# Attention of a transformer block on one core: maxima by query, probabilities by key, sums in column strips, norms once per sequence

## The reference

```python
q, k, v = heads(ln(x) @ Wq), heads(ln(x) @ Wk), heads(ln(x) @ Wv)   # 16 heads of 8 columns
scores = einsum('bhld,bhlwd->bhlw', q, k_win) * 8 ** -0.5            # keys l-63 .. l of each query l
attn = softmax(where(invalid, -inf, scores))
x = x + (einsum('bhlw,bhlwd->bhld', attn, v_win)) @ Wo
xf = ln(x)                                                           # 8192 rows
weights, experts = top_k(softmax(xf @ w_router), 2)                  # 8 experts, capacity 2048, in order of rows
y = gelu(rows_of_expert @ w1[e]) @ w2[e]                             # 128 -> 512 -> 128
out = x + bias + sum_k weights_k * y_k                               # rows over the capacity drop out
```

## Time and profile before

| | us |
|---|---|
| runs | 1155.83, 1158.16, 1158.24 (median 1158.16) |
| profiled execution, its span | 1155.7 |
| TensorE matmul busy in it | 990.6 (86%) |
| VectorE, ScalarE, POOL busy | 644.9, 609.6, 488.5 |
| mean granted TensorE clock | 0.912 |

### The profile page before, as it was taken

One profiled execution on the slowest core, in us unless ns is written; L12 is line 12 of the kernel. 1 busy time (PEld: TensorE's weight loads), 2 busy tenths in 40 slices (PEclk: granted clock), 3 DMA queues, 4 the chain that ended last, 5 costly groups with the idle time before them and its releaser, 6 DMA issues.

```text
span 1155.7 us, 24887 instructions
## 1 busy us (share of the span) xinstructions
PE 990.6 (86%) x7670; PEld 942.3 (82%) x7670; DVE 644.9 (56%) x1980; ACT 609.6 (53%) x1898; POOL 488.5 (42%) x445
## 2 busy tenths in 40 slices
PE   2999998899899889989997998999605998889791
PEld 1899998799799889988997997999604997878691
DVE  5777787488468747856774786578521121212110
ACT  2777676466467647655673765567202442434330
POOL 4122124421712352162135225212531877777777
PEclk9999999799799979988997998899656999889896
DMA  8900001100100110010011001000122455455533
GB/s 186 390 17 18 11 10 47 32 18 18 56 12 9 41 37 9 18 60 17 9 36 42 9 18 56 22 9 31 50 65 87 54 90 90 76 84 89 89 33 34
DMA packets 61821, 60.14 MB, mean 52 GB/s; under 512 B 6721, under 2 KB 50648, under 8 KB 60736
## 3 DMA queue, kind: packets, MB, share of 16 engines
q1 hardware_dynamic: 34944, 40.18, 10.6%
q0 software_dynamic: 22528, 17.22, 10.3%
q10 hardware_dynamic: 4288, 2.10, 1.2%
HBM read 17.70 MB, written 31.59 MB: 43 GB/s over the span
## 4 chain that ended last, share of the span: by engine, by line
PE 44%; issue 18%; POOL 11%; DVE 11%; another core or an unknown queue 6%; ACT 4%; DMA 3%; ACTq 1%; DVEq 1%; POOLq 0%; SPq 0%
PE bank L993 15%; PE bank L1015 11%; POOL out L429 11%; PE bank L1002 8%; PE bank L1029 2%; DMA out<-y_sb,xg 2%; ACT probs L509 2%; ACT kT L479 2%; DVE negmax L661 2%; DVE probsT L666 1%; PE bank L979 1%; PE bank L1021 1%; DVE xn L652 1%; PE bank L973 1%
## 5 line engine op out<-in xcount | busy, mean ns | idle before, releaser
L509 ACT ACTIVATE probs<-bank,negmax 128x128 f32<-128x128 f32 x1036 | 295.2, 368 | 285.2 <-DVE negmax L661 278.4
L360 POOL TENSOR_TENSOR qbd<-qT,quadmask 128x512 f32<-128x512 f32 x132 | 134.5, 1040 | 522.8 <-ACT qT L467 400.3
L993 PE MATMUL bank<-kT,qbd 128*128 (+1 forms) x2072 | 295.1, 289 | 0.0
L993 PEld LDWEIGHTS bank<-kT,qbd 128*128 128x128 f32 x2072 | 273.2, 206 | 0.0
L1015 PEld LDWEIGHTS bank<-v_sb,probsT 128*128 128x128 f32 x2048 | 263.1, 200 | 3.7 <-issue 3.4
L1015 PE MATMUL bank<-v_sb,probsT 128*128 (+1 forms) x2048 | 258.9, 259 | 3.7 <-issue 3.5
L429 POOL DMA_INDIRECT out<-y_sb,xg x128 | 198.2, 1548 | 81.0 <-DVE y_sb L934 42.0
L661 DVE TENSOR_REDUCE negmax<-bank 128x4 f32<-128x512 f32 x259 | 177.9, 687 | 75.5 <-PE bank L993 42.4
L1002 PE MATMUL bank<-ident,probs 128*128 128x128 f32 x1024 | 170.1, 291 | 39.2 <-ACT probsT L515 26.6
L666 DVE COPY probsT<-bank 128x512 f32<-128x512 f32 x192 | 132.5, 690 | 122.7 <-PE bank L1002 76.0
L1002 PEld LDWEIGHTS bank<-ident,probs 128*128 128x128 f32 x1024 | 125.0, 152 | 56.5 <-ACT probsT L515 30.6
(11 more groups left out here) (114 smaller groups left out, 930.6 us busy)
## 6 DMA issues: line engine op xcount, KB each, us to landing
slots_dram<-empty_rows SPq DMA_DIRECT2D x8, 1096.0 KB, 15.4
xg<-slots_dram SPq DMA_DIRECT2D x32, 274.0 KB, 4.3
rows_sb<-xn SPq DMA_DIRECT2D x33, 128.0 KB
out<-xbias SPq DMA_DIRECT2D x32, 128.0 KB
w_sb<-in_L_ffn_w SPq DMA_DIRECT2D x16, 256.0 KB
send_rows<-rows_sb SPq DMA_DIRECT2D x7, 548.0 KB, 3.0
out<-y_sb,xg POOLq DMA_INDIRECT x128
slots_dram<-send_rows,slot_id POOLq DMA_INDIRECT x112
```

The costliest lines, as they stand in the source:

```text
L360: last = pool.tensor_tensor(out=qbd[s][half][:, :, :, :], in0=q.unsqueeze(2).to_broadcast([P, 2, HQ, BLK]), in1=heads.to_broadcast([P, 2, ...
L509: last = nc.scalar.activation(probs[:, k % 4, c, :], scores[k % 4][:, c * P:(c + 1) * P], ACT.Exp, bias=negmax[:, k % 4, c:c + 1])
L993: last = mm(scores[k % 4][:, c * P:(c + 1) * P], qbd[s][half][:, blk, h:h + 2, :].rearrange("p h q -> p (h q)"), keys.rearrange("p o j -> ...
```

## The change

Attention now goes tile by tile (64 slots of 128 rows), and 8 tiles, a whole sequence, form a loop's body.

- Scores are computed twice. `scores` (by query) serves the maxima only: per half of the heads, two bf16 matmuls write the mask (64 rows of contraction, 512 columns), and 8 f32 matmuls with only 32 rows of contraction add the scores; neighbours in the list stand in different strips of 32 rows and write different banks. VectorE takes the maxima of 128 x 1024 in one instruction, negated, and splits them in a bf16 part and a rest (`low_part`); `maxima_T` transposes them, and `maxima_out` copies them to 32 rows of `moving`.
- `scores_T` (by key) makes the scores with keys on the partitions: 8 bf16 matmuls of 96 rows put mask and negated maxima into PSUM, and 4 f32 matmuls of 32 rows and 256 columns add the scores. ScalarE then needs one `Exp` of 128 x 1024 without a bias, and its result needs no transpose: L1002, L666 and L515 are gone.
- `weighted` has the values as stationary operand, 32 columns wide, and 128 moving columns of probabilities; four groups of heads write four strips of 32 partitions. The result is copied by ScalarE (128 x 512) and transposed back by 4 transposes (`weighted_T`).
- The norms are done once per sequence with 16 columns at a time (8 tiles of each norm); POOL does the subtraction and the product (`normed`, `normed_again`). The second norm, the router and the routing of a sequence run within the next one; `rows_sb` holds one sequence, and `keep_rows` is gone.
- `sends`: 4 indirect DMAs in each of the slots 0 to 3, two sequences later. The last two sequences' are sent after the loop.
- VectorE waits for the load of all of x (`ld_x[1]`) ahead of its first maxima.
- The experts' stage keeps its work; its tensors in PSUM have other names.

The diff, cut to its core:

```diff
-            def keep_rows(n):
-                sp.wait_ge(s_xn2, n + 1)
-                sp.dma_start(rows_sb[:, bass.ds(2 * n, 2), 0:D], xn2[:, :, :]).then_inc(s_rows, 16)
...
+            def normed_again(b):
+                pool.wait_ge(s_ln, b + 2)
+                pool.wait_ge(s_send, START + 16 * (b - 1))
+                tiles = x_sb[:, bass.ds((b - 1) * TILES, TILES), :]
+                pool.tensor_tensor(out=rows_sb[:, :, 0:D], in0=tiles,
+                                   in1=mean[:, 0:TILES].unsqueeze(2).to_broadcast([P, TILES, D]),
+                                   op=ALU.subtract).then_inc(s_xd2, 1)
+                pool.wait_ge(s_xd2, b)
+                for h in range(2):
+                    half = slice(4 * h, 4 * h + 4)
+                    pool.tensor_tensor(out=rows_sb[:, half, 0:D], in0=rows_sb[:, half, 0:D],
+                                       in1=rs_y[:, half].unsqueeze(2).to_broadcast([P, 4, D]),
+                                       op=ALU.mult).then_inc(s_xn2, 1)
+            def sends(b, t):
+                if t == 0:
+                    pool.wait_ge(s_send, START + 16 * (b - 1))
+                    pool.sem_inc(s_turn_pool, 1)
+                if t < 4:
+                    send(send_rows, range(2 * t, 2 * t + 2))
+                if t == 5:
+                    pool.wait_ge(s_scat, 16 * TOPK * TILES * (b - 1))
+                    pool.sem_inc(s_sent, 1)
...
-            def exps(n, k):
-                act.wait_ge(s_max, UNITS * n + k + 1)
-                for c in range(4):
-                    last = nc.scalar.activation(probs[:, k % 4, c, :], scores[k % 4][:, c * P:(c + 1) * P], ACT.Exp,
-                                                bias=negmax[:, k % 4, c:c + 1])
-                last.then_inc(s_exp, 1)
...
+            def exps(g, gp):
+                act.wait_ge(s_scoresT, 2 * g + gp + 1)
+                nc.scalar.activation(probsT[:, gp].rearrange("p b k h q -> p (b k h q)"),
+                                     sT_ps[:, :, :].rearrange("p b c -> p (b c)"), ACT.Exp).then_inc(s_exp, 1)
+            def weighted_out(g):
+                act.wait_ge(s_pv, 2 * g + 2)
+                nc.scalar.copy(u_sb[:, :, :].rearrange("p i q -> p (i q)"), u_ps[:, :]).then_inc(s_u, 1)
...
+            def score_max(g, gp):
+                dve.wait_ge(s_scores, 2 * g + gp + 1)
+                nc.vector.tensor_reduce(negmax[:, 0, gp * 8:gp * 8 + 8],
+                                        s_ps[:, :, :].rearrange("p b (c j) -> p (b c) j", c=4),
                                         AX.X, ALU.max, negate=True).then_inc(s_max, 1)
...
+            def low_part(g):
+                dve.wait_ge(s_max, 2 * g + 2)
+                nc.vector.tensor_copy(negmax_hi[:, :], negmax[:, 0, :]).then_inc(d_hi, 1)
+                dve.wait_ge(d_hi, g + 1)
+                nc.vector.tensor_tensor(out=negmax[:, 1, :], in0=negmax[:, 0, :], in1=negmax_hi[:, :],
+                                        op=ALU.subtract).then_inc(s_low, 1)
+            def maxima_out(g):
+                dve.wait_ge(s_maxT, g + 1)
+                nc.vector.tensor_copy(moving[0:STRIP, :, :].rearrange("p h q -> p (h q)"),
+                                      s_ps[0:STRIP, 0, 0:P]).then_inc(s_moving, 1)
...
+            def slot(b, t, chain, route, first=False, last=False):
+                g = b * TILES + t
+                ahead = t + 1 < TILES or not last
+                if ahead:
+                    score_max(g + 1, 0)
+                fill(b, t, 0, chain, route, first, last)
+                if ahead:
+                    score_max(g + 1, 1)
+                    low_part(g + 1)
+                if not (first and t < 2):
+                    residual(g - 2)
+                if not first and t == 5:
+                    logits(b)
+                if not first and t == 7:
+                    positions(route, b - 1, 0)
+                if not (first and t == 0):
+                    normalise(g - 1)
+                if ahead:
+                    maxima_out(g + 1)
+                fill(b, t, 1, chain, route, first, last)
...
-            def score(m, k):
...
-                    pe.wait_ge(s_k_sb, 2 * (m + 1))
-                for c in range(4):
-                    j = 4 * half + c
-                    h = 2 * j % HQ
-                    keys = kT[:, 2 * j // HQ, bass.ds(m % PAIRS_PER_SEQ * 4 + 2 * s + blk, 1), :]
-                    last = mm(scores[k % 4][:, c * P:(c + 1) * P],
-                              qbd[s][half][:, blk, h:h + 2, :].rearrange("p h q -> p (h q)"),
-                              keys.rearrange("p o j -> p (o j)"), start=True, stop=True)
+            def scores(t, gp):
+                masks = window[:, 0:2, :] if t == 0 else window[:, 1:3, :]
+                for b in range(2):
+                    half = slice(b * HALF, (b + 1) * HALF)
+                    mm(s_ps[:, b, :].rearrange("p (k h j) -> p k h j", k=2, h=2),
+                       onehot[half, :, :].rearrange("p h q -> p (h q)"),
+                       masks[half].unsqueeze(2).to_broadcast([HALF, 2, 2, P]), start=True, stop=True)
+                for blk in range(2):
+                    at = (2 * t + blk) * BLK
+                    for p2 in range(2):
+                        for b in range(2):
+                            rows = slice(STRIP * (2 * gp + b), STRIP * (2 * gp + b + 1))
+                            c = 2 * blk + p2
+                            last = mm(s_ps[:, b, c * P:(c + 1) * P],
+                                      qbd[t % 4][rows, blk, 2 * p2:2 * p2 + 2, :].rearrange("p h q -> p (h q)"),
+                                      kT[rows, at:at + P], start=False, stop=True, skip_group_check=True)
                 last.then_inc(s_scores, 1)
...
+            def maxima_T(g):
+                pe.wait_ge(s_low, g + 1)
+                nc.tensor.transpose(s_ps[0:STRIP, 0, 0:P], negmax[:, :, :].rearrange("p a c -> p (a c)"),
+                                    ident[:, :]).then_inc(s_maxT, 1)
+            def scores_T(t, gp):
+                for b in range(2):
+                    for blk in range(2):
+                        for p2 in range(2):
+                            c = 2 * blk + p2
+                            which = gp * 8 + b * 4 + c if t > 0 or blk > 0 else 16 + gp * 4 + b * 2 + p2
+                            mm(sT_ps[:, b, c * P:(c + 1) * P], picks[0:3 * STRIP, which, :],
+                               moving[0:3 * STRIP, :, :].rearrange("p h q -> p (h q)"),
+                               start=(c == 0), stop=True, skip_group_check=(c > 0))
+                for blk in range(2):
+                    at = (2 * t + blk) * BLK
+                    for b in range(2):
+                        rows = slice(STRIP * (2 * gp + b), STRIP * (2 * gp + b + 1))
+                        last = mm(sT_ps[:, b, blk * 2 * P:(blk + 1) * 2 * P], kT[rows, at:at + P],
+                                  qbd[t % 4][rows, blk, :, :].rearrange("p h q -> p (h q)"),
+                                  start=False, stop=True, skip_group_check=True)
+                last.then_inc(s_scoresT, 1)
+            def weighted(t, gp):
+                for blk in range(2):
+                    for c in range(4):
+                        b, p2 = c // 2, c % 2
+                        last = mm(u_ps[STRIP * c:STRIP * (c + 1), (2 * blk + gp) * P:(2 * blk + gp + 1) * P],
+                                  v_sb[:, t // 2, 2 * (t % 2) + blk, 4 * gp + c, :],
+                                  probsT[:, gp, b, blk, 2 * p2:2 * p2 + 2, :].rearrange("p h q -> p (h q)"),
+                                  start=True, stop=True)
                 last.then_inc(s_pv, 1)
-            def context_T(n, s):
-                pe.wait_ge(s_ctx, 2 * n + s + 1)
+            def weighted_T(g):
+                pe.wait_ge(s_u, g + 1)
+                for i in range(4):
+                    last = nc.tensor.transpose(o_ps[:, i * P:(i + 1) * P], u_sb[:, i, :], ident[:, :])
+                last.then_inc(s_uT, 1)
...
+            def slot(b, t, first=False, last=False):
+                g = b * TILES + t
+                ahead, ahead2 = t + 1 < TILES or not last, t + 2 < TILES or not last
+                done = not (first and t == 0)
+                pe.wait_ge(s_moving, g + 1)
+                if done:
+                    pe.wait_ge(s_exp, 2 * g)
+                scores_T(t, 0)
+                if done:
+                    pe.wait_ge(s_exp, 2 * g)
+                    weighted((t - 1) % TILES, 1)
+                if ahead:
+                    pe.wait_ge(s_max, 2 * (g + 1) + 1)
+                    scores((t + 1) % TILES, 1)
+                if not (first and t < 2):
+                    pe.wait_ge(s_ctxT_sb, g - 1)
+                    if t == 5 and not first:
+                        router(b).then_inc(s_lg, 1)
+                    if t == 7 and not first:
+                        counts(b - 1).then_inc(s_pos, 1)
+                    project(g - 2)
```

(50 more changed lines are left out.)

1063 lines of the change are left out of this document (519 added, 544 removed).

## The result

On the machine of the times shown, the changed kernel takes 1197.6 us (median of 4 runs, 1184.9 to 1227.3) against 1158.2 before: a ratio of 1.026, interval [1.023, 1.029]. It is slower, where 1095 and faster was forecast. So each experiment is compared with the kernel before on its own machine. The changed kernel there takes 1143.8, ratio 1.064 [1.062, 1.067]. The kernel before takes 1074.2 to 1075.4 in each of the three series of experiments, so their microseconds can be set side by side to within about 1 us.

A forecast was written before the change was run, and what follows sets the result against it. TensorE was taken to bound attention: 64 tiles at 10.39 us (665) plus 57 at sequence ends made 722, so 1155.7 - 80 + 9 (start) + 8 (end) = 1093 profiled, 1095 median; range 1050 to 1145.

The forecast's parts named there:

- Strips beside each other, factor 2: TensorE's scores, masks and sums: matmuls in different strips overlap by 2, so 9.49 us per tile in place of 15.19.
- rivals 2 and 4: rival 2, and, as number 4, that attention's strips don't run beside each other at all: 1460 us, chance 0.05.
- rival 2: Scores by query: weight loads of row strips don't overlap; 1208 us, chance 0.12; threshold 0.087 us per record.
- rival 1: Attention: sequences' ends flow, or the sums go four abreast; either is -57 us, 1038 us; chance 0.17.
- Changes of shape, 0.085 each: TensorE's switches of array use: ten further ones at 0.085 us, 0.9 us per tile, bounds 0 and 1.7.
- The other engines: Attention, per tile: VectorE about 6.4 us, ScalarE about 4.5; none, POOL included, reaches 10.4.
- rival 3: The round of the score banks decides, held up by TensorE's list: 11.8 us per tile, 1183 us; chance 0.12.
- The start: First maxima wait for the load of x's later rows, at 37 in place of 27.6: +9 us.
- The end: After attention, sends of the last two sequences follow each other: 56 us against 47.6, +8.
- The waits at sequence ends: Attention: of the 114 us standing at sequences' ends, half remains, 57; bounds 0 and 114.
- Rival 5: Attention: small tiles with changes between them leave TensorE at 1.2 GHz for half of it; 1260 us, chance 0.04.
- The chances: Whole kernel: forecast 0.50; faster 0.71, same 0.02, slower 0.27; wider range 1000 to 1210.

The follow-up runs named there:

- e9: The changed kernel with only TensorE's loop over sequences written out, the other four engines' loops kept: 1065.1 us, 0.990 of the kernel before.
- e10: The changed kernel with the loop over sequences written out on the other four engines, TensorE's loop kept: 1144.3 us, 1.063 of the kernel before.
- e6: The changed kernel with 24 extra f32 matmuls over 32 rows of contraction in slot 0 of each sequence: 1238.1 us, 1.136 of the kernel before.
- e2: The changed kernel with 24 extra f32 matmuls over all rows and columns of the array in slot 0 of each sequence: 1163.5 us, 1.081.
- e11: The changed kernel with 24 extra matmuls in slot 0 of each sequence, all 128 rows, in four 32-column strips in turn: 1118.5 us, 1.041.
- e3: The changed kernel with both kinds of scores contracting over all 128 rows, output not the reference's: 1238.6 us (one run).
- e1: The changed kernel with the loop over sequences written out on all five engines: 1053.6 us, 0.982 of the kernel before.
- e7: The kernel before, unchanged, profiled again on a second machine: 1074.2 us, ratio 0.999 to its own runs.

## Why the prediction was wrong, step by step

- **Strips beside each other, factor 2** (against rivals 2 and 4): right. A record of scores by query takes 0.068 us with its group's change of shape in it, under rival 2's threshold of 0.087 and far from one at a time at 0.111. Inside a group the records start in pairs, 0.112 us from pair to pair (307.03, 307.14, 307.25): two abreast. The sums go four abreast, as rival 1 allowed: they start in fours, 0.11 to 0.13 us from four to four (305.92, 306.05, 306.16, 306.27). So the argument that only the second record of one matmul and the first of the next overlap was wrong. With the group's end, 0.036 is 3.1 times 0.111. The Trainium skill (TensorE: Matmul & The Clock Gate, "Measured speedup vs the span model") gives 3.07x for four row strips and 2.38x for three of columns; the trace agrees with its kind of gain, at 3.1 for four of columns in f32.
- **Changes of shape, 0.085 each**: near in sum, by two errors that cancel. The five groups come to 7.20 us where paired rates alone gave 6.68 (1.78 + 0.44 + 0.96 + 1.72 + 1.78). The 0.52 is less than the 0.9 taken, but the sums' gain lies in it too: four abreast their 32 records are 0.88, 0.90 less than the 1.78. Without that, the changes and the ends of groups cost 1.42, some 0.1 to 0.2 for each group, inside the bounds of 0 to 1.7 and half as much again as the 0.9. The tile is 10.01 where 10.39 stood; that it came so near is in part luck.
- **The other engines and rival 3**: right. L647 takes 1.225 us (1.22 forecast) and L504 1.024 (1.01). Undisturbed, TensorE waits for neither.
- **The start**: right, and for the reason given:

```profile
36.10 1.23 DVE L647 TENSOR_REDUCE negmax<-s_ps 128x8 f32<-128x1024 f32 x1 [14.44 <-DMA x_sb<-in_L_attn_x]
```

- **The end**: right in size, 57.3 us from the last sums (851.8) to the first transpose of the experts (909.1), 56 forecast. The order of the sends was as described: the first 16 from 857.5, 6 us behind the last sums, the others from 881.9.

```profile
857.51 0.99 POOL L372 DMA_INDIRECT slots_dram<-send_rows,slot_id  x1 [0.15 <-issue]
...
881.89 0.97 POOL L372 DMA_INDIRECT slots_dram<-rows_sb,slot_id  x1 [4.24 <-issue]
```

- **The waits at sequence ends: this step failed.** As put there: "Bounds for what remains of the 114 us: 0 and 114; I take half, 57, as the bursts remain and the holes' cause isn't shown." Measured: 34.5 us of idle time and 131 of low clock, 166 together, beyond the upper bound. The step took the holes of before for the only ones. It counted the low clock per hole at the price of before, where the clock is back sooner (its longest low stretch in attention is 17.1 us): 54 idle and 48 lost there, under 1 us lost for each idle. Here each of the five holes costs 3.2 itself and 17 by what follows it, 101 in sum. The other 65 are 8.6 of a wait at the start (for the first maxima), 10 of smaller pauses and 46 of low clock away from the returns, of which 19 in the one long stretch behind the router. They are near the 57 forecast for what remains, but the forecast had taken half of an unexplained sum, so that is luck. Two facts were missing, and the trace of before had neither: that the return of a loop eight slots long is a hole of its own (e9, e10), and that a busy TensorE at 1.2 GHz stays there through work over 32 rows (e6), which work over all rows shortens (e2, e11, e3).
- **Rival 5** had the right organ, "the clock stays low", at 0.04 and 1260. Its text set the clock against small tiles as such; for the five long stretches it takes the hole and the small tiles together. In the attention's small tiles without a hole the clock stays up most of the time (e1: 0.98, with short low stretches behind the router alone). But it can also fall without a return: in e6's block with no pause at all, and behind the router or a pause of 0.8 us (e2, e6). So the rival was nearer than its 0.04. The sentence against it, that the low clock stands only behind holes of microseconds, was nearly true (the shortest pause ahead of a fall in the trace of before is 0.9 us), and was no argument, since nobody had asked whether the change makes holes.
- **The chances**: 0.27 for slower came from rivals of price and order, and none had the loop in it. With the returns added, the forecast's own sum of 1093 comes to 1194, against 1187.7 profiled. That the 1197.6 us measured lie inside the range 1000 to 1210 is luck: rivals 2 and 3, whose 1208 and 1183 reach there, didn't happen.

What is still open: why the first machine's kernel before has holes at its bursts; the low stretches behind the router, short in e1 and once 37.5 us long in the changed kernel; and whether rows in use or the share of the array at work is what the clock goes by.

## What to carry to other kernels

When a change makes a loop's body longer, price its return on the bottleneck engine and ask what runs right behind it. Price a hole of TensorE by the work that follows: behind it the clock was low for 27 to 34 us in the changed kernel's own tiles, for 10 to 14 us with a block over all rows put in, and for 3.4 us or not at all with the scores over all rows. If the loop can't be written out, a block over all rows right behind the return can be worth more than it costs (e11, 25 us less). The block of 128 x 128 in e2 cost more than it gave. And a remainder whose cause no row shows is not bounded by its old size.

## What the runs showed of the hardware that I had not expected

- The clock of a TensorE that is busy for 37.38 of 37.40 us can stay at 1.2 GHz all that time, with a block of matmuls over 32 rows (e6), and such a block at full clock was followed by a fall to 1.2 GHz with no pause ahead of it (e6, 138.7); over all rows, 48 records in 2.3 us (e11) or 7.1 us (e2) are followed by, or contain, the rise.
- The return of a loop with 968 matmuls in its body stops TensorE for 2.7 to 3.5 us, around which 16 KB packets of instructions arrive, 11 more in sum than without TensorE's returns (83 against 72); the returns of the kernel before, with 190 in the body, show no hole (e7).
- Records of f32 matmuls start two abreast in two row strips and four abreast in four column strips. With the ends of their groups that is a gain of 1.7 (1.09 us for 16 records against 1.88) and of 3.1 (0.036 us a record against 0.111).
- An unchanged kernel took 1158 us on one machine and 1075 on two others, with a granted clock in attention of 0.94 and 1.00.
